# A graph kernel on one core: the scaled one-hot as a three-operand instruction, a split placing matmul, and the order of layer 2's loads

## The reference, cut to what matters

```python
# layer 1
msg      = x[src] @ W_msg.T + b_msg + edge_embed[clip(edge_type)]
messages = segment_sum(msg, dst);  x = layernorm(x + gru(messages, x))
# layer 2
proj = x @ fc_weight.T;  el = proj[src];  er = proj[dst]
e    = sum(leaky_relu(el + er, 0.2) * a, -1)
gate = sigmoid(sum(el * er, -1))
w    = sigmoid(e * gate)
neigh = segment_sum(x[src] * w[:, None], dst) / max(deg, 1)
x = layernorm(x + (1 + eps) * x + neigh)
```

## Time and profile before

| | |
|---|---|
| median of 3 runs | 2963.24 us |
| the profiled execution's own time | 2978.43 us |
| its span | 2976.6 us |
| DVE busy over the span | 90% |
| POOL busy over the span | 71% |
| PE, PEld, ACT busy over the span | 66%, 57%, 53% |
| granted PE clock, mean | 0.767 of full speed |

### The profile page before, as it was taken

How to read it: one execution, slowest core, us unless ns; L and a number is a source line. 1 busy time by engine, 2 the same in 40 slices (tenths; PEclk the granted TensorE clock), 3 DMA queues, 4 the chain that set the end, 5 groups by cost and what they waited for, 6 DMA issues and landing times. The chain is left out here.

```text
span 2976.6 us, 63843 instructions
## 1 busy us (share of the span) xinstructions
PE 1959.1 (66%) x13872; PEld 1688.4 (57%) x13872; DVE 2691.1 (90%) x13389; ACT 1571.2 (53%) x3622; POOL 2108.7 (71%) x2219
## 2 busy tenths in 40 slices
PE   6999999999945555555555555555555555555554
PEld 3888888887534455444444544544445544544543
DVE  8998998996889999999999989999999999999997
ACT  5877777775544444444444444444444444444445
POOL 2476777766667777777777777777777777777771
PEclk9999999999966766767677677666676676676765
DMA  8233333333354444444444444444444444444442
GB/s 210 61 99 96 98 96 94 100 91 104 106 170 135 135 135 132 139 135 135 135 133 135 138 138 135 131 135 139 137 135 135 135 136 139 135 135 135 139 136 69
DMA packets 241191, 376.21 MB, mean 126 GB/s; under 512 B 109269, under 2 KB 157612, under 8 KB 240428
## 3 DMA queue, kind: packets, MB, share of 16 engines
q0 software_dynamic: 99456, 271.71, 30.9%
q1 hardware_dynamic: 139380, 102.20, 12.3%
q10 hardware_dynamic: 2212, 0.60, 0.1%
HBM read 350.21 MB, written 23.61 MB: 126 GB/s over the span
## 5 line engine op out<-in xcount | busy, mean ns | idle before, releaser
L1619 POOL DMA_INDIRECT got<-rows,idx x1624 | 1564.3, 963 | 506.4 <-issue 477.3
L1824 PE MATMUL sum_ps<-whot,got 128*128 128x128 f32 x3264 | 694.7, 383 | 530.4 <-DVE whot L1631 430.3
L1824 PEld LDWEIGHTS sum_ps<-whot,got 128*128 128x128 f32 x3264 | 599.9, 275 | 609.1 <-DVE whot L1631 483.4
L1817 PE MATMUL er_ps<-win,hot_t 128*128 128x128 bf16 x4932 | 506.1, 277 | 401.2 <-ACT hot_t L1764 379.7
L1817 PEld LDWEIGHTS er_ps<-win,hot_t 128*128 128x128 bf16 x4932 | 450.7, 130 | 450.2 <-ACT hot_t L1764 415.7
L1631 DVE TENSOR_SCALAR whot<-iota_f,dl,w_s 128x128 f32<-128x128 f32 x1632 | 457.8, 362 | 158.7 <-ACT w_s L1769 158.6
L842 POOL DMA_INDIRECT got<-y_rows,idx x448 | 456.9, 1020 | 200.2 <-issue 134.0
L1000 ACT CAST cols<-c_ps 128x318 fp32r<-128x318 f32 x1176 | 493.5, 440 | 144.9 <-PE c_ps L1086 107.0
L1032 PE MATMUL span_ps<-y_parts,cols 128*126 128x256 f32 x2968 | 568.4, 319 | 0.2 <-ACT cols L1000 0.2
L1760 ACT ACTIVATE apart<-dst_b,less 128x512 bf16<-128x512 int16 x406 | 290.0, 714 | 342.3 <-DMA dst_b<-dst_row 336.5
L1032 PEld LDWEIGHTS span_ps<-y_parts,cols 128*126 128x126 f32 x2968 | 453.6, 192 | 5.5 <-issue 1.3
(11 more groups left out here) (256 smaller groups left out, 1829.5 us busy)
## 6 DMA issues: line engine op xcount, KB each, us to landing
dst_b<-dst_row SPq DMA_DIRECT2D x59, 512.0 KB
got<-rows,idx POOLq DMA_INDIRECT x1624
dst_b<-dst_row SPq DMA_DIRECT2D x59, 384.0 KB
win<-parts SPq DMA_DIRECT2D x118, 96.0 KB, 3.7
got<-y_rows,idx POOLq DMA_INDIRECT x448
parts<-split SPq DMA_DIRECT2D x12, 384.0 KB, 3.5
y_rows<-y_parts SPq DMA_DIRECT2D x1, 3584.0 KB, 9.9
rows<-nodes SPq DMA_DIRECT2D x12, 256.0 KB, 2.3
```

Source lines behind the costliest of these rows:

```text
L1619: pool.indirect_dma_start(got[:, c, i, :], None, rows, bass.IndirectOffsetOnAxis(ap=idx1[:, c, i:i + 1], axis=0)).then_inc(gathered[c], 16)
L1817: mm = pe.matmul(er_ps[:, c, i * D:(i + 1) * D], hot_t[:, c, i * P:(i + 1) * P], win[:, int(c >= HALF), part, :], start=(part == 0), stop= ...
L1824: mm = pe.matmul(sum_ps[:, 0:P], got[:, c, i, D:2 * D], whot[:, c, i, :], start=(c == 0 and i == 0), stop=(c == NS - 1 and i == STEP - 1))
```

## The change

1. `weigh` makes each of its four `whot` columns by `scalar_tensor_tensor`: the column number of the edge stays a per-partition scalar, and the weight comes as a second tensor operand that is one value per partition broadcast over 128 elements. Before, it was `tensor_scalar` with two per-partition scalars.
2. `copy_sums` copies the high and the low half by one ACT instruction each, the low one into a float32r tile `turned_lo`; `place` becomes float32r. `post` multiplies the high half as float32, as before, and the low half as float32r.
3. In SP's loop the waits and loads of `dst_b` and `win` of a half come first, and the wait for the half's gathers with the load of `idx1` last.

```diff
-            turned_s = sb("turned_s", [P, 2, YW], F32, ph)
-            place = sb("place", [P, 2, P], F32, ph)
+            turned_s = sb("turned_s", [P, 2, D], F32, ph)
+            turned_lo = sb("turned_lo", [P, 2, D], F32R, ph)
+            place = sb("place", [P, 2, P], F32R, ph)
...
-                        act.copy(turned_s[0:ROWS, h, :], span_ps[0:ROWS, h, 0:YW]).then_inc(s_copied, 1)
+                        act.copy(turned_s[0:ROWS, h, :], span_ps[0:ROWS, h, 0:D])
+                        act.copy(turned_lo[0:ROWS, h, :], span_ps[0:ROWS, h, D:YW]).then_inc(s_copied, 1)
...
-                        for i in range(2):
-                            mm = pe.matmul(out_ps[:, 0:P], turned_s[0:ROWS, h, i * D:(i + 1) * D],
-                                           place[0:ROWS, h, :], start=(i == 0), stop=(i == 1))
-                        mm.then_inc(posted, 1)
+                        pe.matmul(out_ps[:, 0:P], turned_s[0:ROWS, h, :], place[0:ROWS, h, :].bitcast(F32),
+                                  start=True, stop=False)
+                        pe.matmul(out_ps[:, 0:P], turned_lo[0:ROWS, h, :], place[0:ROWS, h, :],
+                                  start=False, stop=True).then_inc(posted, 1)
...
                         for h, c in ((0, HALF - 1), (1, NS - 1)):
-                            sp.wait_ge(gathered[c], 16 * STEP * k + 16 * STEP)
-                            sp.sem_inc(begun, 1)
-                            load_idx(sp, h, edges_next)
                             sp.wait_ge(apart_done, NS * k + c + 1)
                             sp.sem_inc(begun, 1)
                             load_dst(sp, h, col_next)
                             sp.wait_ge(er_done, NS * k + c + 2)
                             sp.sem_inc(begun, 1)
                             load_window(h, at_next)
+                            sp.wait_ge(gathered[c], 16 * STEP * k + 16 * STEP)
+                            sp.sem_inc(begun, 1)
+                            load_idx(sp, h, edges_next)
...
-                            m = dve.tensor_scalar(whot[:, c, i, :], iota_f[:], dl[:, at:at + 1], w_s[:, c, i:i + 1],
-                                                  ALU.is_equal, ALU.mult)
+                            m = dve.scalar_tensor_tensor(out=whot[:, c, i, :], in0=iota_f[:], scalar=dl[:, at:at + 1],
+                                                         in1=w_s[:, c, i:i + 1].to_broadcast([P, P]),
+                                                         op0=ALU.is_equal, op1=ALU.mult)
```

## The result

The kernel after takes 2987.85 us in the median of three runs (2985.59 to 2997.23), against 2963.24: a ratio of 1.0085, 95% interval 1.0058 to 1.0111. It is **slower, by some 25 us**; the forecast was 2952 us. Its profiled execution took 2985.6 us (span 2983.8), close to its median, while that of before lay 15 us above its own, and above all 49 executions of before that were timed later beside the experiments (2960.9 to 2971.9 us). So the two spans differ by 7 us where the medians differ by 25.

What follows compares the result with a forecast made beforehand. POOL's gathers were taken to set layer 2's pace, PE to bound layer 1. Placing -6, head -1.6, end -7.9 and POOL's rate +4 made -11.5 us, off 2963.2 giving 2952 us; range 2928 to 2982, the forecast's own 2939 to 2962.

Steps and rivals of the forecast that it cites:

- The placing: Layer 1 on PE: the low half in one pass instead of two saves 6 us, range 0 to 9.
- The head: Layer 2's first body: earlier dst_b shortens DVE's wait for w_s and POOL's for the sum, 1.6 us (0 to 2.85).
- The end: Last body of layer 2: DVE begins the last chunk when its rows are there, saving 7.9 us (0 to 8.6).
- The one-hot's own price: DVE's three-operand one-hot in layer 2: 0.26 us from start to start, no change, ends 0.21 and 0.39.
- POOL's own rate: Layer 2's gathers on POOL: DVE's disturbance of them changes, costing +4 us, with ends -28 and +78.
- the mark: Mean duration of POOL's gathers, 962 ns before: the forecast is wrong if it is above 980 ns.
- The rival: POOL's gathers get slower, chance 0.20: DVE in step gives 2975 us, new one-hots hitting another gather besides, 3002.
- Its condition: For slower gathers in layer 2: the kernel ends slower once the longer gathers hold 50 us, 0.12 us a chunk.
- the lock-step: Layer 2: DVE would start each chunk a fixed time behind POOL's fourth gather; weighed within the +4 us.
- quicker gathers: Rival, chance 0.12: DVE's new timing or freed ports clear all longer gathers in layer 2, 28 us more, 2920 us.
- the rival in which DVE is the bound: Layer 2, chance 0.05: one-hots from 0.36 us each make DVE set the pace; at 0.39, 49 us, about 2998.

Runs made afterwards that it cites:

- e4: The kernel before with only the change's placing (one pass for the low half, two ACT copies); 2960.5 us, ratio 0.9982.
- e1: The kernel before with only the new three-operand one-hots; 2989.7 us, ratio 1.0079.
- e3: The kernel before with only SP's new order of the loads; 2981.0 us, ratio 1.0056.
- e10: e5 with the one-hots' third operand also read from PSUM, a feature block replacing the weights (output not attention's); 2936.6 us, ratio 0.9909.
- e7: The kernel before with only the scores' input moved from SBUF to PSUM; 2959.0 us, ratio 0.9972.
- e6: e2 with the scores' input moved from SBUF to PSUM; 2955.7 us, ratio 0.9963.
- e5: The kernel after, all three parts, with the scores' input moved from SBUF to PSUM; 2988.9 us, ratio 1.0065.
- e8: e6 with the count of near rows moved to the start of DVE's chunk; 2952.9 us, ratio 0.9968.
- e11: The kernel before with the change's placing and the scores read from PSUM, old loads and one-hots kept; 2952.1 us, ratio 0.9962.
- e2: The kernel after with the old one-hots back, new placing and order of the loads kept; 2975.0 us, ratio 1.0034.
- e9: e2 with the count of near rows moved from the end of DVE's chunk to its start; 2965.4 us, ratio 0.9997.

## Why the prediction was wrong

By its own steps:

- **The placing** was to give 6 us and gave 8.8: layer 1's last added sum ends that much earlier (728.88 against 737.71 us in the timeline). A step of PE fell from 0.95 to 0.79 us, and 56 x 0.16 = 9.0. I had put a pass at 0.11 us; taking one off gave 0.16, the upper end of my range (0 to 9 us). Placing instructions are 168 (112 and 56), as told. The second copy on ACT cost nothing that PE shows. A single trace is a rough measure of it: layer 2's first gather stands at 850.4 to 852.5 us in the four kernels with the old placing and at 839.0 to 845.4 in the nine with the new, 8.8 apart in the mean.
- **The head** was to give 1.6, and no run shows that it did. DVE's wait of 1.61 us for `w_s` is 0.81 now. POOL's wait of 2.85 us at 888.85 is 1.86, but it is 1.96 in e4 too, which keeps the old order of the loads, and over the kernels it goes from 1.0 to 4.4 us. The 0.9 us that the first gather gains beyond the 8.8 lie ahead of these waits and inside the spread just named.
- **The end** was to give 7.9 and gave 7.3. The mechanism is right in every row: `dst_b` comes earlier, `apart` waits for it at chunk 1 of the body and no longer at chunk 4, DVE's stall for `w_s` is gone, and the last chunk begins 3.5 us after the last gather.
- **The one-hot's own price** was to stay at 0.26 us from start to start. It is (1.12 - 0.34) / 3 = 0.26. DVE did not become the bound.
- **POOL's own rate** is the step that failed: I took +4 us, and it was +24 in the profiled executions (2085.2 - 2061.0) and some +42 by the medians (below). The mean of a gather, which the prediction had named as the row to decide, is 979 ns over the span and in the stretch, just under the 980 I had set as the mark. The rival had been written down at 0.20 with its two prices, 2975 and 3002; the measured 2988 lies between them. It named both causes: DVE in step with the gathers, and the new form hitting them besides. Its condition held: the excess over 945 ns is 55.5 us, above the 50 I had worked out. Its shares did not: it put 55 us on the gathers beside the scores and 27 on those beside the one-hots, and the kernel after has 15 and 39. That 2988 lies between its two prices is in part luck.

Two things led me to +4. I said that the new form "may disturb more" than the old and put no term on it, although the only rows of an instruction with two SBUF tensors showed a longer gather; e1 prices it at 24 us. And I held the lock-step to be as likely a gain as a loss; e3 is 15 us slower though its end gained 7, so it cost some 22.

The profiled execution of before misled besides. Its excess is 29.6 us, and from it I took the 28 us that quicker gathers could save. If the median run of before had the same head, pace and end (850.4, 2031.4 and 65.2 us, and 1.8 around the span), its excess would be only 2963.2 - 1.8 - 850.4 - 2031.4 - 65.2 = 14 us. By the medians POOL's rate then cost 24.6 + 9.7 + 7.3 = 42 us, near the 24 + 22 that e1 and e3 cost it singly. That the one execution held more long gathers than the median run is an inference, since only one execution has a trace. e10 supports it: it saves 26 us on the kernel before, of which the placing and the end are some 16, which leaves 10 or 11 for the gathers, and not 28.

Two small sums of the prediction are off, and nothing hung on them: 0.27 x 406 less 28 is 82 and not 78, and the rival in which DVE is the bound comes to 2963.2 - 15.5 + 49 = 2997 and not 2998.

## What to carry to other kernels

Where POOL issues indirect gathers at the bound, count the inputs in SBUF of every instruction that DVE runs beside them. Here moving one operand to PSUM gained 8 us (e7) and 20 us (e6), while the new form of the one-hot saved DVE nothing that counted and cost 24; its broadcast column was not free. An engine whose wait is taken away meets the bounding one at other moments, and they can be worse ones: price that meeting before the wait that went away. Take the pace from the mean of the bounding instruction, not from its median, and ask first whether the traced execution is a typical one.

## What the runs showed that I had not expected

- Layer 2's time above the steady pace is such hits. Without them (e10) the 1623 steps from gather to gather take 2031.6 us, 1.252 us each, against 1.285 in the kernel after; 946 ns and 0.305 us give the same.
- A few hits are large: in e5 27 gathers take over 1.3 us, up to 1.8, and hold 16 of its 58 us of excess; in e10, e7, e8 and e11 no gather does but, in e7, the layer's first. What makes one hit so large wasn't worked out.
- The same program varies, perhaps with them: ten runs of e2 went from 2964.95 to 2986.72 us, four of e10 from 2931.8 to 2938.6. Only one of each has a trace.
- Where a delay is taken away, another can take its place in full: in e5 14 us went at the scores and 18 came at the one-hots.
- The order of 0.67 us of work in a chunk of 5 us moved the whole by 10 us (e9 against e2). How the phases of the two engines fall, and why e3's fall so badly, wasn't worked out.
